# Fourier operator and ViT block: ten mode transfers on three issuing engines, and two idle products instead of three

## The reference

```python
x = coords @ fc0_w + fc0_b
for sw, cw, cb in ((sw0, cw0, cb0), ..., (sw3, cw3, cb3)):
    x_ft = rfft2(x)                                   # 20 x 20 modes are kept
    out  = einsum('bixy,ioxy->boxy', x_ft[:, :, :20, :20], sw)
    x1   = irfft2(out into zeros)
    x2   = einsum('bchw,oc->bohw', x, cw) + cb
    x    = gelu(x1 + x2)
x = gelu(x @ fc1_w + fc1_b) @ fc2_w + fc2_b
# then: layernorm, banded attention of 8 heads, layernorm, top-6 of 64 experts, layernorm
```

## Time and profile before

| | us |
|---|---|
| median of 3 runs | 1129.65 |
| lowest and highest | 1129.07, 1131.33 |
| the profiled execution, device time | 1131.64 |
| span of its trace | 1129.8 |
| mean granted TensorE clock in it | 0.978 of full |
| PE busy | 1024.6 (91%) |
| DVE busy | 614.7 (54%) |
| ACT busy | 410.1 (36%) |
| POOL busy | 137.2 (12%) |

### The profile page before, as it was taken

How to read it: one execution, slowest core, us unless ns; L and a number is a source line. 1 busy time by engine, 2 the same in 40 slices (tenths; PEclk the granted TensorE clock), 3 DMA queues, 4 the chain that set the end, 5 groups by cost and what they waited for, 6 DMA issues and landing times.

```text
span 1129.8 us, 36328 instructions
## 1 busy us (share of the span) xinstructions
PE 1024.6 (91%) x16860; PEld 654.0 (58%) x16860; DVE 614.7 (54%) x773; ACT 410.1 (36%) x554; POOL 137.2 (12%) x127
## 2 busy tenths in 40 slices
PE   4899899899989999999899899889999899689996
PEld 3676567567657633676576667567325788632221
DVE  2258455825844221458248455923144577769887
ACT  2332233223223486232232233223585778421100
POOL 6000000000000000000000000020000665334421
PEclk9999999999999999999999999999999899879998
DMA  5220130022021300310220130020011000000000
GB/s 187 89 75 3 62 94 12 3 89 75 3 74 53 115 6 22 118 32 3 89 75 3 44 103 21 3 90 16 2 25 43 1 1 2 2 1 1 1 10 10
DMA packets 25660, 46.75 MB, mean 41 GB/s; under 512 B 9437, under 2 KB 10488, under 8 KB 24869
## 3 DMA queue, kind: packets, MB, share of 16 engines
q1 hardware_dynamic: 24694, 43.49, 12.6%
q10 hardware_dynamic: 384, 0.66, 0.2%
q0 software_dynamic: 432, 0.29, 0.1%
HBM read 30.25 MB, written 10.89 MB: 36 GB/s over the span
## 4 chain that ended last, share of the span: by engine, by line
PE 69%; DVE 14%; issue 6%; ACT 4%; DMA 3%; POOL 2%; SPq 1%; ACTq 0%; POOLq 0%; DVEq 0%
PE PSALL L1288 22%; PE PSALL L1256 7%; DVE WORK L1494 6%; PE PSALL L1366 4%; PE PSALL L1279 4%; PE PSALL L1232 4%; PE PSALL L517 4%; PE PSALL L1151 3%; PE PSALL L1376 3%; PE PSALL L1165 3%; PE PSALL L420 3%; DMA WORK<-MIXED 2%; PE PSALL L505 2%; DVE WORK L1513 2%; PE PSALL L399 2%
## 5 line engine op out<-in xcount | busy, mean ns | idle before, releaser
L1513 DVE STREAM_TRANSPOSE WORK<-PSALL 128x1024 f32<-128x1024 f32 x128 | 152.4, 1230 | 292.9 <-PE PSALL L1256 292.9
L1288 PEld LDWEIGHTS PSALL<-EW,WORK 64*128 64x128 f32 x4096 | 250.0, 193 | 65.5 <-issue 48.3
L1288 PE MATMUL PSALL<-EW,WORK 64*128 64x128 f32 x4096 | 266.1, 283 | 12.8 <-DVE WORK L1513 12.8
L1416 ACT ACTIVATE X<-PSALL,TABLES 128x1024 f32<-128x1024 f32 x128 | 141.7, 1114 | 331.6 <-PE PSALL L1288 331.6
L1494 DVE STREAM_TRANSPOSE WORK<-PSALL 128x1024 f32<-128x1024 f32 x84 | 102.3, 1223 | 26.8 <-PE PSALL L1151 26.8
L1397 ACT COPY SPEC<-PSALL 128x400 f32<-128x400 f32 x64 | 53.9, 851 | 152.7 <-PE PSALL L1165 149.8
L1165 PEld LDWEIGHTS PSALL<-TABLES,WORK 128*64 128x64 f32 x2000 | 67.0, 138 | 65.7 <-DVE WORK L1494 53.2
L1165 PE MATMUL PSALL<-TABLES,WORK 128*64 128x64 f32 x2000 | 80.7, 228 | 23.1 <-DVE WORK L1494 19.9
L1485 DVE STREAM_TRANSPOSE WORK<-X 128x1024 f32<-128x1024 f32 x78 | 92.8, 1207 | 16.4 <-PE PSALL L1288 16.4
L1151 PE MATMUL PSALL<-WORK,DW 32*64 32x256 f32 x2496 | 95.8, 391 | 0.0
L697 POOL MEMSET SW<- 64x4160 f32 x1 | 3.6, 3559 | 725.0 <-PE PSALL L1240 725.0
(11 more groups left out here) (156 smaller groups left out, 1059.1 us busy)
## 6 DMA issues: line engine op xcount, KB each, us to landing
SW<-in_spec_w SPq DMA_DIRECT2D x160, 80.0 KB, 2.7
spec_scr<-MIXED SPq DMA_DIRECT2D x24, 400.0 KB, 3.3
SPEC<-spec_scr SPq DMA_DIRECT2D x32, 200.0 KB
WORK<-spec_scr SPq DMA_DIRECT2D x16, 200.0 KB
WORK<-MIXED SPq DMA_DIRECT2D x64, 40.0 KB
WORK<-in_coords_w SPq DMA_DIRECT2D x2, 1024.0 KB, 4.8
XC<-in_coords_c SPq DMA_DIRECT2D x2, 1024.0 KB, 7.2
hid_scr<-WORK SPq DMA_DIRECT2D x64, 8.0 KB
```

Of the source, the lines that this page charges most:

```text
L1288: m = pe.matmul(PS[2 * p + z][:, 2 * b * GRID:(2 * b + 2) * GRID], G[64 * z:64 * z + 64, n % 2, b, h:h + 4, :, c].rearrange("p q o -> p (q ...
L1416: nc.scalar.activation(X[:, n].rearrange("p b (z d) c w -> p d z b (c w)", z=2)[:, p, :, :, 2 * t * GRID:2 * (t + 1) * GRID], PSALL[:, 2 * ...
L1513: nc.vector.transpose(G[:, n % 2, 2 * x + y].rearrange("p h o v -> p o h v"), PSALL[:, 4 + 2 * x:6 + 2 * x, :].rearrange("p k (h o v) -> p ...
```

## The change

The ten transfers of group 0 are dealt out anew. SP issues `x` = 0 of slices 0 to 3, and `x` = 1 of slice 4. ACT issues `x` = 0 of slice 4. POOL issues `x` = 1 of slices 0 to 3, in a loop over passes and layers that stands between its tail weight loads and `tail_pool`; it counts them on a semaphore of its own, `pool_straight_in`. PE before the first inverse rows, and DVE before it writes over `MIXED`, wait for that semaphore too. `keep_busy(3)` becomes `keep_busy(2)`. What is computed stays the same.

```diff
@@ the counts
-        straight_in = Count(sem("first_modes_copied"), 1, unit=16 * 2 * KXD)
+        straight_in = Count(sem("first_modes_copied"), 1, unit=16 * (KXD + 1))
+        pool_straight_in = Count(sem("first_modes_copied_by_pool"), 1, unit=16 * (KXD - 1))
@@ SP, layer
                 for d in range(KXD - 1):
                     turn.wait(mix_ready, -(-(d + 1) * KYG // 4))
-                    for x in range(2):
-                        straight(sp, d, x)
+                    straight(sp, d, 0, straight_in)
                 turn.wait(mix_ready, N_MIX)
+                straight(sp, KXD - 1, 1, straight_in)
@@ PE, inverse_rows, and DVE, pixels_onto_partitions (k == 0)
                     turn.wait(straight_in, 1)
+                    turn.wait(pool_straight_in, 1)
@@ PE, layer
-                keep_busy(3)
+                keep_busy(2)
@@ ACT, mixed
-                for x in range(2):
-                    straight(act, KXD - 1, x)
+                straight(act, KXD - 1, 0, straight_in)
@@ POOL, behind the tail weight loads
+            turn = Steps(pool)
+            for p in range(PASSES):
+                for l in range(LAYERS):
+                    if l == 0 and p:
+                        pool.wait_ge(ho_out.sem, p * ho_out.stride)
+                    for d in range(KXD - 1):
+                        turn.wait(mix_ready, -(-(d + 1) * KYG // 4))
+                        straight(pool, d, 1, pool_straight_in)
+                    turn.next()
```

More of the change, by code:

```diff
@@ L311, in vit_kernel, with straight @@
         PTP = PSALL[:, 4:6, 0:4 * TOK]
-        def straight(eng, d, x):
+        def straight(eng, d, x, count):
             at = 64 * x + RI * B4 * d
@@ L317, in straight @@
                           MIXED[NG * x:128:2 * NG, d * MODES * CH:(d + 1) * MODES * CH]
-                          ).then_inc(straight_in.sem, 16)
+                          ).then_inc(count.sem, 16)
         def tail_sync(sp):
```

## The result

The changed kernel took 1120.76 us (median of 4 runs, 1118.56 to 1123.91), the kernel before 1130.33 beside it. The ratio is 0.9918 with a 95% interval of 0.9891 to 0.9945, so the change gives 9.3 us, between 6.2 and 12.3. A second group of runs gave 0.9919 (0.9891 to 0.9946). The forecast was 6.3 less than before and 1123.3 us; the time lies in the stated range, but by only 0.2 us: its lower end is 1120.6. The median of the second group was 1123.06, beside 1131.52 for the kernel before.

A forecast was written before the change was run, and what follows sets the result against it. SP's queue of issues plus one landing was taken to bound each layer's first inverse rows. Gains of 6.67 less 0.32 for the added wait, say 6.3, took 1129.65 to 1123.3 us, range 1120.6 to 1127.2.

The forecast's parts named there:

- The bound: Ahead of each layer's first inverse rows: SP's queue of issues plus one landing sets their start.
- ACT's first issue of 1.52: Pass 0, layer 0: this issue, 0.91 longer than an ordinary one, delays its own landing; layer gain taken as 0.87.
- the landing term: Last pair from SP and ACT, issued when all copies are made: lands in 2.95, as old pairs in ordinary layers.
- The twice as large gain of pass 1, layer 0: Pass 1, layer 0: last issue moves by 1.64, gaining 1.41, about twice what the ordinary layers do.
- The added wait: PE's extra semaphore before the first inverse rows: costs 0.04 in each of eight layers, 0.32 in total.
- The idle product: PE ahead of the inverse rows: two products end under the landing and cost nothing; three would leave only 0.29 of 0.70.
- rival 3: A longer PE pause ahead of the inverse rows lowers the clock, 1.56 per layer: 1135.8 us; chance 0.04.
- Rival 1: PE's wait for `pool_straight_in`: POOL issues slowly and lands last; at 2 us an issue, 1139.5 us; chance 0.08.
- Never the releaser: Sign for POOL's four issues per layer, at most 0.73 each: none of them is what PE's wait ends on.
- the 1.1 spare: POOL's fourth transfer lands by 332.7, the new pair at 333.76, so POOL may be 1.1 late for nothing.
- Rival 2: DMA engines, not issues, bound the straight transfers, so the landing does not move: 1129.65 us within 1 us; chance 0.11.

The follow-up runs named there:

- ACT both: The changed kernel with ACT issuing both transfers of d = 4, one behind the other, SP and POOL four each: 1137.12 us, ratio 1.0046.

## Why the prediction was right, and where it was off

**The bound was read rightly.** SP's queue of issues set the landing, and taking it away moved the last issue to t0: in the two traces of the changed kernel every DMA piece starts there, or with POOL's fourth. Putting an issue behind t0 again (ACT both) brought the old stage back, 32.4 against 32.6, though part of that is the longer landing. Single slips of SP in other versions show the same: issues 1.1 and 0.77 late started the inverse rows 0.7 and 0.6 late.

**The size was too small, 6.35 for 8.97.** That is more than the 8.5 which the prediction gave as the most that the change could bring, with every landing at 2.72; the measured time is in the range because this allowed 0.5 more for the clock, and so by some luck. Half of the missing 2.6 is layer 0 of pass 0. The step that failed is that ACT's first issue of 1.52 delays its own landing by 0.91: it is again 1.48 long in the changed kernel, yet PE goes on 2.92 after its start, as in the others, and the version with one product, which lets the landing be seen, has it at 2.83. The long first issue held back what stood behind it in the queue, which was the second transfer, and that is now SP's. The gain of this layer was put at 0.87 and measured 2.15: 0.91 of the difference is that delay, the rest the landing. (In the two versions in which the stores started at t0 ACT's first did land late, at 3.58 and 3.88, but so did its ordinary one of 0.64 in layer 2, at 3.51 and 3.75.) Most of the other half is the landing term. I carried over 2.95, the landing of the old pairs, and the new ones take 2.76 or 2.77 in ordinary layers. A pair does cost 0.3 to 0.4 more than one alone (2.37). But the old pair was not a pair: SP and ACT had each issued another 0.65 before it, four within 0.7 us. That is the likely reason for the 0.2 between them; it was not tried by itself. The Trainium skill, "DMA: Bandwidth & Descriptors", section Rules for kernel authors, says that spreading over SP, ACT and GpSimd "only saves sequencer issue time"; the runs agree for the larger part, 0.7 of the 0.9 per ordinary layer, and show 0.2 beyond it.

**The twice as large gain of pass 1, layer 0** did not come: it is 1.22 against 0.9 on average in the ordinary layers, a third more. The issue moved as forecast, by 1.64, but its landing takes 3.18 instead of 2.95, and 3.11 in the second trace of the change. SP and POOL issue their first four in a burst there, behind the wait for the hidden store; that this is the reason is not shown.

**The added wait** was set at 0.32 in total and cannot be seen: landing to start takes 0.09 now, 0.13 or 0.14 before.

**The idle product** did what was said, and more. That it costs nothing and lets the other gain through is shown by the third product (a stage of 27.3 against 23.7). But what the products are for was not in my sum: old queues with two products are 5.3 us slower than before, 1.0 of it in the stage and most of the rest by the clock. In the change the pause is shorter than before, 0.33 on average against my 0.5, so rival 3 stayed away; it is true of its neighbours. Its chance of 0.04 was too low for a kernel that lies between two versions in which it decides, and the argument that layer 0 had stood for 1.5 us without a fall was weak: behind a pause of over 1 us a fall comes in about half of the layers (12 of 24 in three kernels), not in each.

**Rival 1** did not hold: an issue on POOL takes 0.56, and it lands in 2.6 to 2.9. "Never the releaser" was wrong, though. In two of the sixteen layers of the change, both in its second trace, POOL's fourth landed last, 3.56 and 3.68 after its issue, against my 2.9 at most, so that of the 1.1 spare nothing was left. The cost there was 0.1 to 0.2. **Rival 2** did not hold: the start of the inverse rows moved in every layer, by 0.64 us or more.

## What to carry over

When a wait ends with the last of several small transfers, count the issues on the queue and not the bytes: 0.6 us each here, and it was mostly the moment of the last one and what was issued just ahead of it that mattered. Leave the queue some slack, since a single issue can take 0.5 longer. Idle work that fills a wait has to be cut together with the wait, to end just under the landing: longer takes back the gain, shorter risks the clock; and of the two edits the new queues alone gave 5.3 of 9.0 us of the stage, the shorter idle work alone a loss. A price read from a row belongs to the situation of that row: a long first issue delays its followers, and a pair with two more ahead of it need not land like a pair.

## What the hardware showed that was not expected

A pause of PE of over 1 us ahead of the inverse rows was often followed, a few microseconds later, by a granted clock of 0.50 for 3.4 us, twice that and once three times, at a cost of about 2.1 for a double one. It came behind 12 of 24 such pauses in the three kernels with the most, and behind 2 of 7 in the other traces; behind 2 of 8 of 0.7 to 1.0 us, none of 8 of 0.5 to 0.7, and one of 56 below 0.5. The same transfer mostly landed in 2.37 us with no other straight one near it, 2.77 in a pair, 2.95 with two more just ahead, and 3.1 to 3.2 with a store of 400 KB issued 0.7 ahead of it. In kernels in which POOL issues too, single landings at the same place were up to 1.2 us later than in other layers of the same trace, from ACT and SP as well as from POOL. In the trace before, the ordinary layers stayed between 2.92 and 3.09. Of the six from ACT or SP that took 3.5 to 3.9 by the chains, five are in the two versions whose first store starts at t0 together with ACT's last transfer, and none is in the ordinary layers of the version that holds the stores back. What makes them late is open.
